# A fused attention and ternary-weight feed-forward layer: the order of the first loads, the place of the shift rows in the DMA queue, and the slot of the fourth weight piece

## What is computed

```
qkv  = x @ Wqkv + bqkv                # q: 16 heads of 16; k, v: 4 groups of 16, tiled over the heads
att  = softmax(q k^T / 16) v @ Wout + bout
x1   = layernorm(x + att)
gu   = x1 @ ternary(w_gate_up)^T      # 2048 x 256 weights
h    = silu(gate) * up ;  hn = rms_norm(h)
out  = layernorm(x1 + hn @ ternary(w_proj)^T)
```

## Time and profile before

| | |
|---|---|
| median of 3 runs | 569.85 us (569.84 to 571.31) |
| the profiled execution's own time | 570.28 us |
| its span, first to last instruction | 568.3 us |
| PE busy | 524.5 us, 92% |
| DVE busy | 442.4 us, 78% |
| ACT busy | 366.0 us, 64% |
| POOL busy | 335.5 us, 59% |
| mean granted TensorE clock | 0.984 of full |
| DMA | 49.16 MB, mean 86 GB/s |

### The profile page before, as it was taken

One profiled execution on the slowest core, in us unless ns is written; L12 is line 12 of the kernel. 1 busy time (PEld: TensorE's weight loads), 2 busy tenths in 40 slices (PEclk: granted clock), 3 DMA queues, 4 the chain that ended last, 5 costly groups with the idle time before them and its releaser, 6 DMA issues.

```text
span 568.3 us, 13548 instructions
## 1 busy us (share of the span) xinstructions
PE 524.5 (92%) x4148; PEld 444.7 (78%) x4148; DVE 442.4 (78%) x1002; ACT 366.0 (64%) x738; POOL 335.5 (59%) x517
## 2 busy tenths in 40 slices
PE   4687999899999999999999999999999999999883
PEld 4677778688888888888888888888888888777772
DVE  6876796868888897878787888888888878775764
ACT  4553765466676777676767667676767675667663
POOL 4566764245556656574756656556556565656764
PEclk9896999999999999999999999999999999999998
DMA  8867163536162626354454535262627062010001
GB/s 227 140 142 123 56 125 76 104 71 110 52 116 60 125 30 145 54 126 73 105 96 100 96 89 107 74 115 63 119 37 155 10 152 48 21 40 1 19 20 37
DMA packets 83379, 49.16 MB, mean 86 GB/s; under 512 B 39680, under 2 KB 83328, under 8 KB 83328
## 3 DMA queue, kind: packets, MB, share of 16 engines
q1 hardware_dynamic: 81584, 48.00, 41.0%
q10 hardware_dynamic: 1744, 0.53, 0.4%
HBM read 33.29 MB, written 14.68 MB: 84 GB/s over the span
## 4 chain that ended last, share of the span: by engine, by line
PE 47%; POOL 19%; issue 15%; DVE 10%; ACT 3%; DMA 3%; SPq 1%; ACTq 1%; POOLq 0%; DVEq 0%
PE ffn_ps L588 12%; PE short_ps L514 8%; PE pv_ps L616 7%; PE short_ps L560 6%; PE exp_ps L569 5%; PE down_ps L601 5%; POOL sq_sum L1015 5%; POOL h_lo L1010 4%; POOL rstd L999 2%; DVE row_max L834 2%; DVE h_f L910 2%; DVE gated L903 2%; POOL attB L403 1%; POOL k_p L1034 1%; DMA q_st<-shift_lo 1%
## 5 line engine op out<-in xcount | busy, mean ns | idle before, releaser
L834 DVE TENSOR_REDUCE row_max<-short_ps 128x2 f32<-128x512 f32 x256 | 174.0, 682 | 60.6 <-PE short_ps L560 60.0
L1010 POOL TENSOR_TENSOR h_lo<-h_f,h_hi 128x256 fp32r<-128x256 f32 x128 | 94.5, 739 | 179.7 <-ACT h_hi L737 179.5
L761 ACT ACTIVATE probs<-exp_ps 128x1024 f32<-128x1024 f32 x128 | 130.7, 1021 | 44.5 <-PE exp_ps L569 43.9
L560 PE MATMUL short_ps<-k_st,q_st 65*128 65x256 f32 x512 | 108.5, 296 | 3.6 <-DVE row_max L834 3.3
L746 ACT ACTIVATE tanh<-ffn_ps 128x256 f32<-128x256 f32 x120 | 45.7, 381 | 96.9 <-PE ffn_ps L588 96.9
L560 PEld LDWEIGHTS short_ps<-k_st,q_st 65*128 65x128 f32 x512 | 88.5, 193 | 15.1 <-issue 2.4
L588 PE MATMUL ffn_ps<-x1T_hi,wguT 128*128 128x256 f32 x480 | 80.8, 291 | 9.9 <-DVE h_f L910 9.3
L569 PE MATMUL exp_ps<-q_st,k_st 67*128 67x512 f32 x256 | 81.6, 400 | 3.3 <-DMA q_st<-shift_lo 3.2
L601 PE MATMUL down_ps<-wpT,h_hi 128*128 128x256 f32 x256 | 79.2, 332 | 3.7 <-POOL h_lo L1010 3.5
L588 PE MATMUL ffn_ps<-x1T_lo,wguT 128*128 128x256 f32 x480 | 78.0, 285 | 0.2 <-DVE x1T_lo L823 0.2
L588 PEld LDWEIGHTS ffn_ps<-x1T_hi,wguT 128*128 128x128 f32 x480 | 65.1, 189 | 16.0 <-issue 10.9
(11 more groups left out here) (104 smaller groups left out, 831.2 us busy)
## 6 DMA issues: line engine op xcount, KB each, us to landing
q_st<-q_dram SPq DMA_DIRECT2D x128, 128.0 KB, 4.1
q_dram<-q_p SPq DMA_DIRECT2D x16, 512.0 KB, 3.0
k_st<-k_dram SPq DMA_DIRECT2D x64, 64.0 KB, 2.3
res<-in_L_attn_x_dram SPq DMA_DIRECT2D x16, 256.0 KB, 2.9
out_dram<-y_out SPq DMA_DIRECT2D x16, 256.0 KB, 2.9
xn<-in_L_attn_x_dram SPq DMA_DIRECT2D x62, 64.0 KB, 2.6
wgu_raw<-in_L_ffn_w_gate_up_dram SPq DMA_DIRECT2D x8, 256.0 KB, 6.4
k_dram<-k_p SPq DMA_DIRECT2D x16, 128.0 KB, 2.6
```

Of the source, the lines that this page charges most:

```text
L560: last = pe.matmul(bank[:, t * S:(t + 1) * S], q_st[0:PAD, st.par, head, t * P:(t + 1) * P], k_st[0:PAD, st.par, st.s % 4, :], start=True, ...
L761: act.activation(probs[:, st.s % 4], exp_ps[:], ACT.Exp).then_inc(exp_done, 1)
L834: dve.tensor_reduce(row_max[:, st.par, head * TT:(head + 1) * TT], short(n, f"max{i}")[:].rearrange("p (t k) -> p t k", t=TT), AX.X, ALU.m ...
L1010: pool.tensor_tensor(h_p[1][:, st.s % 4, :], h_f[:, st.s % 2, :], h_p[0][:, st.s % 4, :].bitcast(F32), ALU.subtract).then_inc(h_lo, 1)
```

## The change

Constants: `LOAD_X` -8 to -7; piece 3 is read in slot 8 and made in slot 9 and each later piece two slots later than before (the last is made in slot 25 and turned in slot 28); `W_POOL_FROM` 4 to 3. On ACT the load of wqkv is issued first and one x block after it; SP issues three x blocks instead of two. In SP's slot the load of x moves behind the shift rows, and the half-0 queries of element 1 move from slot 11 to slot 13, behind the shift rows. On DVE the turning of x (all elements but the first) moves to the end of the slot.

```diff
-LOAD_X = -8
+LOAD_X = -7
-W_READ = (1, 2, 3, 5, 8, 10, 12, 14, 16, 18, 20, 22)
+W_READ = (1, 2, 3, 8, 10, 12, 14, 16, 18, 20, 22, 24)
-W_TURN = (5, 8, 9, 10, 12, 14, 16, 18, 20, 22, 24, 26)
+W_TURN = (5, 8, 9, 12, 14, 16, 18, 20, 22, 24, 26, 28)
-W_POOL_FROM = 4
+W_POOL_FROM = 3
...
         @block.sync
-            for group in range(2):
+            for group in range(3):
                 load_blocks(sp, Step(0, 0, None), group)
...
-                if st := n.once(STACK_QK):
+                if (st := n.once(STACK_QK)) and not (st.it is None and st.b == 1):
...
-                if (st := n.once(LOAD_X)) and not (st.it is None and st.b < 2):
-                    sp_wait(xT_made, st.count(1, -1))
-                    for group in range(P // BLOCK):
-                        load_blocks(sp, st, group)
...
                                 .bitcast(F32), shift_p[half][part][:].bitcast(F32)).then_inc(shift_loaded[half], 16)
+                if n.it is None and n.t == SHIFT_T[0]:
+                    sp.wait_ge(q_saved[1], 16)
+                    stack_queries(Step(1, 0, None), 0)
+                if (st := n.once(LOAD_X)) and not (st.it is None and st.b < 2):
+                    sp_wait(xT_made, st.count(1, -1))
+                    for group in range(P // BLOCK):
+                        load_blocks(sp, st, group)
...
         @block.scalar
-            for group in range(2, P // BLOCK):
-                load_blocks(act, Step(0, 0, None), group)
             act.dma_start(wqkv[:], Wqkv.rearrange("(t p) n -> p t n", p=P)).then_inc(wqkv_loaded, 16)
+            load_blocks(act, Step(0, 0, None), 3)
...
         @block.vector
+            def turn_x(st):
+                wait(dve, x_loaded[st.par], st.count2(64, 64))
+                wait(dve, k_made, st.count(1, 0))
+                dve.transpose(xT[:].rearrange("p k t -> p (k t)"),
+                              xn[:, st.par].rearrange("p k n j -> p (k n j)")).then_inc(xT_made, 1)
...
-                if st := x_turn(n):
-                    wait(dve, x_loaded[st.par], st.count2(64, 64))
-                    wait(dve, k_made, st.count(1, 0))
-                    dve.transpose(xT[:].rearrange("p k t -> p (k t)"),
-                                  xn[:, st.par].rearrange("p k n j -> p (k n j)")).then_inc(xT_made, 1)
-                    if st.it is None and st.b == 0:
-                        dve.memset(q_st[SROWS:PAD, 0].bitcast(F32), 0.0).then_inc(q_zeros[0], 1)
+                if (st := x_turn(n)) and st.it is None and st.b == 0:
+                    turn_x(st)
+                    dve.memset(q_st[SROWS:PAD, 0].bitcast(F32), 0.0).then_inc(q_zeros[0], 1)
...
+                if (st := x_turn(n)) and not (st.it is None and st.b == 0):
+                    turn_x(st)
```

## The result

The change made the kernel slightly slower: median 571.17 us against 569.88 us for the kernel before on the same chip, ratio 1.0023 with a 95% interval of 1.0012 to 1.0034. The forecast was 564.8 us (range 562.7 to 567.7), faster than before. The profiled execution after took 570.99 us, its span is 569.0 us, its mean granted clock 0.986.

The account below looks back on a forecast made before the run. PE was taken as the bound from 140 us on, so only the start-up could win: 3.2 + 2.6 + 1.2 - 1.7 - 0.2 = 5.1 us, from a median of 569.85 to 564.8 us (range 562.7 to 567.7).

Parts of the forecast that it names:

- First loads: Start-up: wqkv issued first, x whole near 5.2, PE starting near 6.1, 1.5 us earlier; keys' and queries' save gains 0.3.
- the start-up wins little: Rival, chance 0.11: wqkv and x hold each other up, slot 9 gains only 0.5 us; total 568.6.
- Slot 9, 3.2 us: Without the fourth piece in slot 6, idle products begin near 20.8; slot 9 starts at 26.2 instead of 29.40.
- Shift rows, 2.6 us: Before slot 15's exponential scores: shift rows issued ahead of element 1's queries land in time, ending PE's wait of 2.57 us.
- The clock behind it, 1.2 us: Behind slot 15's scores: no 1.2 GHz stretch, DVE next to limit; wins 1.2 us (0.3 to 1.6), slots 17 to 24 7.0 earlier.
- The piece in slot 25 and its turning, -1.7 and -0.2: The piece before DVE's shift rows in slot 25 costs 1.7 us (1.0 to 2.2); the turning in slot 28 costs 0.2.
- a rival of its own, at 0.19: Rival, chance 0.19: at slot 25 the clock falls, losing 1.7 us more, and 1.0 at slot 31; total 567.4.
- The loop, 0: Loop: earlier keys, later x load and DVE's swapped turn bring 0 us (-0.5 to +1.0 over all elements).
- Slot 31, 0: POOL's later low queries of element 3 could add up to 1.0 us at slot 31; taken as 0.
- it wins more: Rival, chance 0.10: slot 9 gains 3.9, slot 25 loses 1.0, the loop saves 0.5; total 562.9 us.
- the prediction's expectation: At slot 25: PE's new idle time, 1.7 us and 0.3 before, is under 2.57, so no clock fall is expected.

Follow-up runs that it names:

- L: Part of the change: the new order of the first loads (wqkv first on ACT, three x blocks on SP); alone on the kernel before, ratio 1.0006.
- e4: Kernel before with only the weight pieces moved to their new slots: 573.84 us, ratio 1.0078 to the kernel before.
- e7: Changed kernel with the zeroing of one q_st row done by POOL instead of DVE: 569.00 us, ratio 0.9985 to the kernel before.
- e14: Changed kernel with the weight pieces back at their old slots: 567.11 us, ratio 0.9935 to the kernel before.
- e15: Changed kernel with the old order of first loads and the weight pieces at their old slots: 567.73 us, ratio 0.9933 to the kernel before.
- e12: Changed kernel with old first loads, weight pieces at old slots, and zeroing of one q_st row on POOL: 567.34 us, ratio 0.9951 to the kernel before.
- S: Part of the change: half-0 queries of element 1 moved behind the shift rows; alone on the kernel before, ratio 0.9990.
- e3: Kernel before with only the half-0 queries of element 1 moved behind the shift rows: 569.29 us, ratio 0.9990.
- e2: Changed kernel with the old order of the first loads: 569.73 us, ratio 1.0000 to the kernel before.
- T: Part of the change: the turning of x moved to the end of DVE's slot; no run has it alone.
- e5: Kernel before with only the x load moved one slot later and behind the shift rows, DVE's turning unchanged: 569.40 us, ratio 1.0002.
- e11: Kernel before with only the zeroing of one q_st row given from DVE to POOL: 570.14 us, ratio 0.9997.
- e9: Changed kernel with the last weight piece read in slot 26, made in 27, turned in 29: 570.19 us, ratio 1.0006 to the kernel before.
- X: Part of the change: the x load moved behind the shift rows (LOAD_X -7); alone on the kernel before, ratio 1.0002.
- e1: Kernel before with only the new order of the first loads: 570.11 us, ratio 1.0006.
- e8: Changed kernel with the old order of first loads and the zeroing of one q_st row on POOL: 569.20 us, ratio 0.9959 to the kernel before.
- e6: Changed kernel with the half-0 queries of element 1 back in slot 11, ahead of the shift rows: 572.49 us, ratio 1.0049 to the kernel before.
- e10: Kernel before with element 0's first shift rows issued by ACT on its own queue: 570.78 us, ratio 1.0016.

## Why the prediction was wrong, step by step

**First loads: failed, at the bound.** x whole at 5.2 and PE at 6.1 were expected; x was whole at 6.33. I let the x blocks land 3.1 us after their issue with 384 KB of wqkv now ahead of them; they took 3.8 to 4.2. That is the condition of the rival "the start-up wins little", at 0.11. The save of the keys was to gain 0.3, with a bound of 0 to 1.0, which had no loss in it: it lost 1.4 in the profile. In the total time L costs nothing with the pieces at their old slots and 0.2 to 0.3% with the pieces moved, since only then slot 9 follows the save.

**Slot 9, 3.2 us: failed, the largest miss.** The idle products began earlier and at full clock, if only at 22.58 and not at 20.8, and the step itself names the wait that comes next. That wait was mis-sized: the fourth query load was issued at 23.1, not at 21.3, for the late save, and took 6.0 us, not 4.9; 1.8 and 1.1 of the 3.1 us that are missing. The longer load is not chance: it is there in every kernel with moved pieces, also where the save is early (e4, e7), and the wait of 2.1 to 2.5 us with it. The step took the duration of the load as given, while with the piece moved a packet of instructions falls into it. In e4, from the same save as before, slot 9 gained 1.8. And the idle time before slot 9, which the step left at 0.7 us (25.5 to 26.2) and gave no price, became 2.53 and cost the clock behind it: 1.1 us by slot 11, of which 0.8 were back by slot 13.

**Shift rows, 2.6 us: right.** From slot 9 to the exponential scores of slot 15 after wins 2.4; each row landed 1.85 us after its issue.

**The clock behind it, 1.2 us: failed.** First it came true (the exponential scores of slot 16 were 4.41 ahead, two more than those of slot 15), then slot 17 waited 2.40 us for the key stack, and the clock fell at 54.4. The sentence that failed is that the queries "land by 47.5" and that the x load's leaving frees the way. Queries and keys, eight loads issued without a gap from 44.3, landed at 53.6: the keys took 3.2 to 4.7 us each, before 2.3 to 2.5, with the DMA share at 0.56 when their issue began. The last key load landed 1.95 us after the third with an instruction packet (8 KB, at 51.3) under way; in e14, e15 and e12 this packet comes after the keys have landed, and the last load 0.7 to 1.0 us after the third. As at slot 9 this is a coincidence, not a test. S moves the queue, it doesn't empty it: e3 has the same wait at 1.1. Without the pieces (e14) PE arrives at slot 17 a microsecond later and waits 0.2; both together win 3.1 at slot 19 where after has 1.5. What the clock takes there e2 shows: it has the same two waits (2.4 and 2.3 us), its clock stayed full behind both, and it lost nothing from slot 17 to 19 (2.82 and 3.04 ahead), where after lost 0.9 (2.38 and 1.52).

**The piece in slot 25 and its turning, -1.7 and -0.2: near for the piece, with a term beside it that was missing.** In after the way from slot 25 to 27 costs 2.5 us. 1.0 of it, from slot 25 to 26, e14 has as well, without a piece there, and so have all kernels with T; those without T (e3, e4, e5, e11) haven't. So it goes with DVE's later turn of x, which I had priced at 0; no run has T alone. In the ten profiles with T one DVE instruction of slot 25 (`attB`) takes 0.87 us, in the seven without it 0.42: 0.45 of the 1.0, and why is open. The piece's own share is 1.5, and 0.3 for the turning, near the forecast. In e4 and e2 4.2 and 3.2 us went from slot 26 to 27, with the clock. That was a rival of its own, at 0.19; its mechanism is shown (e4, e2), though not in the profile of after.

**The loop, 0: right** (e5). **Slot 31, 0: right in the change**, but it is where the cover is thinnest (e9).

What was wrong in common: I priced each piece of work where it was taken away and where it was put by its path in one trace, and took the gain of slot 9 as passed on rigidly. The time between the keys' save and slot 9 belongs to a chain of transfers (14.5 to 26.6 us before; 15.9 to 29.1 after). DVE, POOL and ACT could do a weight piece in it at nearly no cost; every later slot has DVE near its limit. None of the three terms 3.2, 1.2 and -1.9 alone explains the miss: 3.1 us are missing at slot 9, another 2.3 by slot 24 (3.8 expected, 1.5 got); from slot 24 to 32 -1.9 was expected and -1.6 came, and that it came so near is luck: 0.85 us of it are slot 31, where the profile before had its shift rows late and nearly every other one hadn't. Two rivals had a true part each, the late x and the price of slot 25; I never added them up.

Three small slips in the working change nothing: the fourth query load before landed at 26.6, not 26.5; a mean clock of 0.67 is two thirds of the time at 1.2 GHz, not half; the terms of "it wins more" give 7.0, not 6.9. And PE's waits from 106 us on name h_lo (2.0 us) beside h_f.

**What stays open.** Why S and X alone give 0.6 us and nothing (both inside the interval), and S, X and T together 3.8 (e15), isn't settled. In e3 the x load stands ahead of the key stack (51.60), in e15 behind it (48.66), and from slot 9 to 19 e15 wins 3.0 us where e3 wins 1.8; that accounts for a part and is argued from two profiles. By its profile e15 gains 1.5 us in all, by its ratio 3.8, by its median against the other groups' some 2: the kernel before had a median of 571.34 in that group and 569.35 to 569.88 in the others. The profiles don't help with the size either: those of e1, e7, e8, e9, e11 and e15 are of the slowest of their runs, those of e4 and e6 of the fastest. So the sign of e15 and e14 is sure, their size is not to better than about 2 us. Whether the instruction packets are what makes the two stacks late is open too; a run that moves one of them alone would tell.

## What to carry to other kernels

Before taking work out of a stretch, ask which transfer the stretch waits for anyway: an engine's idle time of 5 us after the move (a bracket in the timeline) says that the work may have been free where it was. Moving a small transfer ahead of large ones pays at once and is charged to the next large one; follow the queue to the last transfer before writing down a gain. Look, too, whether another transfer, even one of instructions, now falls into the stretch. And where a sum rests on when the first loads land, take it from several executions: here these differ by 1.8 us, more than most terms of the sum.

## What the runs showed of the hardware

Loads of 16-partition stacks from DRAM are slow together: while they are in flight the DMA engines are fully busy (share 1.1 and more) at 115 to 160 GB/s, and each of the eight takes 3.2 to 5.6 us to land (queries and keys of element 1 in after), where the four key loads of the kernel before took 2.3 to 2.5. Small rows on another queue behind them took 5.9 us (e10), ahead of them 1.8. The window is from after, PE waiting for the keys:

```profile
52.00:54.00 2.00, 0.35 (x3) 0.35 (x4) 1.41 (x3) 1.19 (x3) 1.84 (x3) 1.00 1.14 134
```

After an idle time of PE of 2.2 to 2.5 us the clock fell to 1.2 GHz in after (twice) and in e4's slot 26, and not behind e12's wait of 1.6 us at 52.2. But it stayed full in e2 behind 2.40 us (to 29.3) and 2.35 (to 53.2). Behind the 1.3 us in slot 26 it fell in e2 and stayed in after, and in e14 it fell at 47.1 behind one of 1.16. So the length of the gap alone doesn't decide, and the prediction's expectation that less than the 2.57 us of the earlier trace rows leaves the clock alone was wrong. The Trainium skill ("TensorE: Matmul & The Clock Gate", the part on the clock gate) has the gate's look-out run free of the kernel; these runs agree with that, in that the same wait is followed by the fall in one execution and not in another, but they don't show it by themselves.
